# Projections of a chunk in another order, two roots by ACT, and row maxima of the second attention by differences of key blocks

## The reference

```
x = norm(x + attn0(x))      # 16 heads of 64, causal, softmax(q k / 8)
x = norm(x + ffn0(x))       # silu(x w1) * (x w2), two 512x512 layers with gelu, w3
x = norm(x + attn1(x))      # 16 heads of 8, no mask, a Gaussian bias on the scores
x = norm(x + x W^T + b + x (low-rank weight)^T)
```

```
c = tanh(mq @ wfq + bfq + (mean(mq) @ wfg + bfg));  P = 2048 * sigmoid(sum(c*up));  Z = 2048 * sigmoid(sum(c*uz))
G = -2 (j - P)^2 / Z^2                     # for key position j, per head and query
probs = softmax(q k / sqrt(8) + G);  ctx = probs v
```

## Time and profile before

| | |
|---|---|
| median of 3 runs | 1779.66 us (1779.0 to 1783.94) |
| the profiled execution | 1781.96 us, span 1780.2 us |
| PE busy | 1620.0 us (91%) |
| DVE busy | 1313.4 us (74%) |
| ACT busy | 983.8 us (55%) |
| POOL busy | 719.3 us (40%) |

### The profile page before, as it was taken

One profiled execution on the slowest core, in us unless ns is written; L12 is line 12 of the kernel. 1 busy time (PEld: TensorE's weight loads), 2 busy tenths in 40 slices (PEclk: granted clock), 3 DMA queues, 4 the chain that ended last, 5 costly groups with the idle time before them and its releaser, 6 DMA issues. The chain is left out here.

```text
span 1780.2 us, 28289 instructions
## 1 busy us (share of the span) xinstructions
PE 1620.0 (91%) x10680; PEld 477.6 (27%) x10680; DVE 1313.4 (74%) x2616; ACT 983.8 (55%) x1168; POOL 719.3 (40%) x462
## 2 busy tenths in 40 slices
PE   7899999999999999995988579999999999999995
PEld 3232333333332323222444211111111111111122
DVE  6767576666667575723555589999999999999964
ACT  2444545544545544442545306777777777777774
POOL 4577887878787878895222110000000000000012
PEclk8999999999999999996999758999999999999998
DMA  5100000000000000001012430111211121111000
GB/s 113 37 8 13 14 13 8 13 14 7 19 8 19 8 13 14 13 13 26 8 36 58 128 68 1 24 24 24 46 30 31 30 39 24 24 24 24 2 2 24
DMA packets 76217, 46.42 MB, mean 26 GB/s; under 512 B 22158, under 2 KB 74930, under 8 KB 76082
## 3 DMA queue, kind: packets, MB, share of 16 engines
q1 hardware_dynamic: 74738, 43.38, 11.4%
q10 hardware_dynamic: 1344, 1.25, 0.2%
HBM read 25.66 MB, written 9.31 MB: 20 GB/s over the span
## 5 line engine op out<-in xcount | busy, mean ns | idle before, releaser
L1899 DVE TENSOR_REDUCE maxpart<-ps_r 128x1 f32<-128x512 f32 x1024 | 634.4, 682 | 24.8 <-PE ps_r L1757 23.1
L1716 ACT ACTIVATE probs<-ps_e 128x1024 f32<-128x1024 f32 x512 | 504.8, 1023 | 193.1 <-PE ps_e L1785 187.9
L369 POOL TENSOR_TENSOR acc<-acc,probs 128x1024 f32<-128x1024 f32 (+3 forms) x256 | 503.2, 1965 | 77.6 <-ACT probs L422 56.1
L422 ACT ACTIVATE probs<-ps_e 128x1024 f32<-128x1024 f32 (+1 forms) x320 | 285.7, 901 | 371.0 <-PE ps_e L591 124.9
L1757 PE MATMUL ps_r<-krows,qrows 60*128 60x512 bf16 x1024 | 346.8, 402 | 50.5 <-DVE maxpart L1899 17.9
L608 PE MATMUL ps_o<-probs,v 128*64 128x512 f32 (+3 forms) x1280 | 307.6, 559 | 0.2 <-ACT pv_raw L429 0.2
L1681 POOL TENSOR_TENSOR rstd<-veps,power 128x4 f32<-128x4 f32 x8 | 8.1, 1012 | 698.5 <-DVE veps L1949 698.5
L698 DVE TENSOR_REDUCE maxpart<-ps_x 128x2 f32<-128x1024 f32 x192 | 234.5, 1221 | 74.7 <-PE ps_x L516 74.7
L1785 PE MATMUL ps_e<-qrows,krows 62*128 62x512 bf16 x1024 | 278.6, 386 | 2.3 <-ACT probs L1716 0.9
L1795 PE MATMUL ps_o<-probs,v 128*9 128x512 f32 x2048 | 269.5, 598 | 12.4 <-ACT probs L1716 12.3
L1757 PEld LDWEIGHTS ps_r<-krows,qrows 60*128 60x128 bf16 x1024 | 79.9, 94 | 468.2 <-DVE maxpart L1899 352.6
(11 more groups left out here) (305 smaller groups left out, 1396.1 us busy)
## 6 DMA issues: line engine op xcount, KB each, us to landing
qrows<-q_rows SPq DMA_DIRECT2D x64, 192.0 KB
rbc<-rden SPq DMA_DIRECT2D x128, 64.0 KB, 2.1
q_rows<-parts_q SPq DMA_DIRECT2D x24, 128.0 KB, 2.3
k_rows<-parts_k SPq DMA_DIRECT2D x24, 128.0 KB, 2.3
krows<-k_rows SPq DMA_DIRECT2D x16, 192.0 KB, 5.4
w_rows<-parts_w SPq DMA_DIRECT2D x6, 256.0 KB, 2.6
qrows<-a_rows SPq DMA_DIRECT2D x64, 24.0 KB
qrows<-w_rows SPq DMA_DIRECT2D x64, 24.0 KB
```

The lines of the kernel that those rows point to most:

```text
L369: pool.tensor_tensor(acc[:, u % 2, :, o:], acc[:, u % 2, :, o:], probs[:, turn % RING, :, o:], ALU.add)\
L422: act.activation(probs[:, turn % RING, :, o:], ps_e[:, turn % 2, :, o:], ACT.Exp, scale=1.0 / math.sqrt(D0))\
L1716: act.activation(probs[:, HG * (turn % 2) + hh], ps_e[:, e % 2], ACT.Exp).then_inc(s_ex, 1)
L1899: dve.reduce_max(maxpart[:, at:at + 1], ps_r[:, k, :], AX.X).then_inc(s_bf[k], 1)
```

## The change

1. **Projections.** The four projections of a chunk run in the order q, k, f, v in place of q, k, v, f. q stands ahead of `hidden(c, 1, (0, 1))`, k behind it, f behind the third block of that layer, and v behind the fourth. ACT empties q ahead of the first gelu of the layer and f ahead of the last. DVE takes `value` behind the last `hidden_low`, not ahead of it.
2. **Roots.** For the first layer norm of the stage and the last one, ACT takes a square root (`square_root`) and DVE the reciprocal of it, in place of POOL's power. The other six norms of the stage keep POOL.
3. **Maxima.** For chosen pairs of key blocks A = b (upper rows) and B = b + 1 (lower rows), PE computes q (kA - kB) in one matmul over 124 rows, with `nrows` holding kA and -kB; ACT writes relu of it to `over`; DVE adds `over` to the scores of B and takes the maximum in one instruction (`tensor_tensor_reduce`), since max(A, B) = B + relu(A - B). Blocks 8 to 71 of the stretch before the first turn are all paired (32 pairs); from then on the first of the four pairs of each turn (119 turns). In a turn the blocks go in the order 0, 2, 3, 1, 4, 5, 6, 7, where 0 is the difference and 1 the block that joins it; ACT's relu stands behind the exponential of head 0.
4. **What that needs.** The 4 unused rows of `qrows` and of `nrows` are set to 0 by 4 DMAs each from a row that DVE clears; `nrows` is filled by ACT (negation, 60x4096) and POOL (copy) for the first head group, and by POOL (both) for the other three; `maxpart` is set to -3e38 once. The low-rank weight's copies on ACT stand between the relus.

The core of the diff:

```diff
-        J_AT = {(kind, c): 4 * c + n for c in range(NQ) for n, kind in enumerate("qkvf")}
+        J_AT = {(kind, c): 4 * c + n for c in range(NQ) for n, kind in enumerate("qkfv")}
...
                 if c + 1 < NQ:
                     to_tokens("n0", c + 1)
+                if c > 0:
+                    project("q", c - 1)
                 hidden(c, 1, (0, 1))
                 if c > 0:
-                    project("q", c - 1)
                     project("k", c - 1)
                 hidden(c, 1, (2,))
                 if c + 1 < NQ:
                     to_features("n0", c + 1)
                 if c > 0:
-                    project("v", c - 1)
+                    project("f", c - 1)
                 hidden(c, 1, (3,))
                 if c > 0:
-                    project("f", c - 1)
+                    project("v", c - 1)
...
+            def square_root(n):
+                act.wait_ge(s_ve, n + 1)
+                act.activation(root[:, :], veps[:, :], ACT.Sqrt).then_inc(s_rt, 1)
...
+                if (name, c) in (("n0", 0), ("n1", NQ - 1)):
+                    link(dve.reciprocal(rstd[:, :], root[:, :]))
...
                 hidden_low(c, 1, 2)
                 if c > 0:
                     key(c - 1)
+                hidden_low(c, 1, 3)
+                if c > 0:
                     value(c - 1)
-                hidden_low(c, 1, 3)
...
-            return [("max", b) for b in range(first, min(first + LEAD, NU * BU))]
+            return [("max", first + n) for n in (0, 2, 3, 1, 4, 5, 6, 7) if first < NU * BU]
...
+        DIFF = {b: n for n, b in enumerate([b for b in range(2 * NC, BU + LEAD) if b % 2 == 0] +
+                                           [b for b in range(BU + LEAD, NU * BU) if b % (2 * NC) == 0])}
...
+            def positive(b):
+                n, (k, m) = DIFF[b], RING_OF[b]
+                act.wait_ge(s_bp[k], m + 1)
+                if n >= 2:
+                    k1, m1 = RING_OF[JOINS[n - 2]]
+                    act.wait_ge(s_bf[k1], m1 + 1)
+                act.activation(over[:, n % 2, :], ps_r[:, k, :], ACT.Relu).then_inc(s_bf[k], 1)
...
+            act.wait_ge(s_k[0], 16 * NQ)
+            rows = slice(64, 64 + R_M)
+            act.activation(nrows[rows, 0], krows[rows, 0], ACT.Copy, scale=-1.0).then_inc(s_neg, 1)
...
                 for hh in range(HG):
                     exps(HG * turn + hh)
+                    for op in TURNS[turn][2 * hh:2 * hh + 2]:
+                        if op[0] == "max" and op[1] in DIFF:
+                            positive(op[1])
...
+                    return pe.matmul(out, qrows[0:64 + R_M, u % 3, c, hh, t * P:(t + 1) * P],
+                                     nrows[0:64 + R_M, u // NQ % 2, hh, c * KB:(c + 1) * KB], start=True, stop=True)
...
+                    dve.tensor_tensor_reduce(out=larger[:, n % 2, :], in0=ps_r[:, k, :], in1=over[:, n % 2, :], scale=1.0, scalar=-3e38,
+                                             op0=ALU.add, op1=ALU.max, accum_out=maxpart[:, at:at + 1]).then_inc(s_bf[k], 1)
```

More of the change, by code:

```diff
@@ L881, in build @@
         power = sb("power", [P, 4])
+        root = sb("root", [P, 4])
         rstd = sb("rstd", [P, 4])
@@ L999, in _ @@
                 sp.dma_start(end_w[n][:, :], a[f"L1_{src}"].rearrange("(a n) -> a n", a=1).to_broadcast([P, DM])).then_inc(s_ew, 16)
-            sp.wait_ge(s_cr, 5)
+            sp.wait_ge(s_cr, 6)
+            for row in range(R_M, 64):
+                sp.dma_start(qrows[row:row + 1].rearrange("a u c h (x n) -> a (u c h x) n", n=KB),
+                             zrow[0:1, :, :].to_broadcast([1, 3 * 2 * HG, KB])).then_inc(s_z, 16)
             n_d = 0
@@ L1523, in build @@
         rowmax = sb("rowmax1", [P, HG * 4], F32)
+        nrows = sb("nrows", [P, 2, HG, HALF], BF16)
+        over = sb("over", [P, 2, QC], F32)
+        larger = sb("larger", [P, 2, QC], BF16)
         maxhl = sb("maxhl1", [P, 2, 2, HG * 4], BF16)
@@ L1552, in build @@
         s_bf = [sem(f"s_bf1{k}") for k in range(3)]
+        s_neg = sem("s_neg1")
+        s_cpy = sem("s_cpy1")
         s_rm = sem("s_rm1")
@@ L1627, in _ @@
         def _(sp):
+            for row in range(R_M, 64):
+                sp.dma_start(nrows[row:row + 1].rearrange("a b h (c n) -> a (b h c) n", n=KB),
+                             zrow[0:1, :, :].to_broadcast([1, 2 * HG * HALF // KB, KB])).then_inc(s_z, 16)
             load_g(sp, 1)
@@ L1670, in _ @@
             pool.tensor_tensor(w_t[:, :], w_t[:, :], w_d[:, :], ALU.add).then_inc(s_wt, 1)
+            pool.wait_ge(s_wt, 1)
+            pool.wait_ge(s_xb, NQ)
+            for g in range(1, NG):
+                negate_k(g)
+                copy_k(g)
             steps = [0]
```

62 lines of the change are left out of this document (51 added, 11 removed).

## The result

The changed kernel takes 1766.65 us (median of 4 runs, 1765.82 to 1767.26), the kernel before 1779.34 beside it. The ratio is 0.992, 95% interval 0.9905 to 0.9935: 13 us faster, clear of the 0.3% (5.3 us) that the prediction takes for the least that can be told from no change. The forecast was 1746.6 and its range ended at 1766.0. The sign was right; the size was off by a factor of 2.6.

What follows compares the result with a forecast made beforehand. It took a chain over PE, DVE and ACT, not DVE's amount of work, to bound steady turns. Terms -17.9 - 1.2 - 3.5 - 10.5 = -33.1 on 1781.96 gave 1748.9, less 2.3 for the median 1746.6 us; range 1732 to 1766.

Steps and rivals of the forecast that it cites:

- Projections, -17.9 forecast: Ffn stage: PE's waits for the readers of v and q go, and most of the half clock behind them: -17.9 us.
- Roots, -1.2: First and last layer norm: root and reciprocal at 0.4 replace POOL's 1.01 us power, 0.6 saved twice: -1.2 us.
- part 3: Maxima ahead of the first turn: 28 pairs save 0.16 us each, weight copies take about 1.0 back: -3.5 us.
- The turns, -0.7 a unit: Ring turns: turn 7 and turns 0 to 2 together give -0.7 us a unit, in 15 units -10.5 us.
- the steady chain: Turns 3 to 6: a chain over PE, DVE and ACT sets 5.16 us a turn and keeps all links, so no gain.
- Turn 7's -0.6: End of a unit: one maximum less before the copy of the transposed maxima, so the DMA starts 0.6 us earlier.
- the -0.1 of turns 0 to 2: Start of a unit: DVE no longer decides, but ACT is nearly full and turn 2's equal rows pair less well: -0.1 us.
- Rival A: Units give nothing: ACT's relu costs in turns 0 to 2 what turn 7 gains; -22.6, 1757 us; chance 0.17.
- Rival C: Turns: PE pays for full rows and equal halves side by side, 0.2 us in 119 turns, 1770 us; chance 0.09.
- Rival B: Turns: DVE decides after all, every turn shrinks by 0.45 us, 54 us more gain, 1703 us; chance 0.06.
- D: Turns: DVE waits for the relu and the ring falls behind, +36 on -22.6, slower at 1793 us; chance 0.06.
- E: Ffn stage: projections give a third, their wait replaced by one for `key`; -21, 1758 us; chance 0.08.

Runs made afterwards that it cites:

- e1: The kernel before with the new order of the projections alone: 1763.32 us, ratio 0.9886.
- e2: The kernel before with the two roots by ACT alone: 1783.65 us, ratio 1.0009.
- e8: The changed kernel with a one-column exponential on ACT ahead of the relus, to load its table early: 1763.11 us, ratio 0.9896.
- e7: The changed kernel with the bf16 identity written by ACT, ahead of its negation, in place of DVE's cast: 1763.21 us, ratio 0.9895.
- e9: The kernel before with each turn's first block over full rows, zeros for the negated keys, no relu or join, identity by ACT: 1787.31 us, ratio 1.0031.
- e6: The changed kernel with a turn's blocks in the order 0, 3, 2, 1, 4, 5, 6, 7: 1762.48 us, ratio 0.9891.
- e10: The kernel before with the second half of `pv` ahead of the fifth block in each turn: 1790.27 us, ratio 1.0048.
- e12: The changed kernel without turn 2's difference, identity by ACT, exponential's table early, second half of `pv` ahead of the fifth block: 1762.83 us, ratio 0.9896.

## Why the prediction was wrong

The time is 20.0 us above the forecast. Of these, 16.9 stand in the profiled execution (16.8 by the landmarks): 13.0 in the turns and 4.9 ahead of them, less 1.1 that the ffn stage gave more. The other 3.1 are no mechanism: the profiled execution of the kernel before was 2.3 above its median, which the forecast took off again, and the changed kernel's was 0.8 below.

1. **Projections, -17.9 forecast.** e1 alone has 20.0 at the gate product, counted from the start of the stage, and a first block of the ring 19.1 earlier. The mechanism and the places were right. The clock's fall went away whole; I had left 0.7 of it.
2. **Roots, -1.2.** Each step is 0.63 shorter, as taken, but that is not the stage: up to the gate product e2 keeps 0.01 of it, and the changed kernel is 0.7 ahead of e1. The added loads lie in idle time. The Trainium skill's higher price for a switch (ScalarE: Activation LUTs, What ACT_TABLE_LOAD costs) is not borne out here: the load at tanh starts 0.02 us after the activation ahead of it ends, is 1.28 long, and is followed by the next activation 0.01 later (981.42 to 982.71 in the changed kernel), and nothing waits for it. What I missed belongs to the relus of part 3: the change also moves a load that was there before, the exponential's, from idle time to between a relu and an exponential: 0.9 us of turn 0 (e8).
3. **Ahead of the first turn, -3.5; measured +1.4.** The failed sentence is "Filling `nrows`, on ACT and on POOL, is done beside the first eight blocks". In the changed kernel it is done before them, at 1013.28, and PE's first block starts at 1013.40: a DVE cast of 0.21 us stands still during POOL's copy, and PE waits for the cast, 2.7 us (e7). The first block comes 1.9 us late by it, as that sentence priced a late fill, but by another route. The pair's pitch was right, and by the chain named; the weight steps took 1.7 of it back and not "about 1.0". Up to the first split the balance is +0.3, and 1.1 more are lost from there to the first `pv`, 0.9 of them by the exponential's load (e8).
4. **The turns, -0.7 a unit; measured +0.17 (by the mean unit; the turns as a whole scatter by more, see above).** The claim that the steady chain keeps its links held: 5.16 before and after, with DVE idle. Turn 7's -0.6 came out as -0.4: its first step is 0.52 shorter, and the next, which the DMA ends, some 0.1 longer. The failed term is the -0.1 of turns 0 to 2, which measured +0.56. It took DVE, which runs there without a gap, for the engine that sets their length; with a maximum less for DVE in each, turns 0 and 1 are as long as before (8.61 against 8.59), and turn 2 is longer. The sentence on equal rows priced the pairing at nearly nothing. In turn 2, which has no wait to hide it, the full-row difference costs 0.31 (e9) and the blocks 3 and 1 of equal halves 0.22 (e6). Over 15 units this term is 9.9 us off, turn 7 another 3.

The range was also drawn too narrow for its own sum: the bounds of the four parts add up to 1728 and 1780, and the text has 1733 to 1762 without saying how. The time lies 0.65 us above the range.

Rival A had the right outcome (the units give nothing), and the wrong cause: in the turns of a unit ACT's relu costs nothing that the runs show, since e9 has the same 0.31 without it. Rival C had the right cause at the wrong place: full rows cost their slot once a unit, in turn 2, not in 119 turns, because a steady turn has the wait for the bank to hide them. What it quotes from the Trainium skill (TensorEngine Tiling (Array Packing), Key Properties) is borne out that far: the trace shows a full-row matmul start only near the end of the half-row ones (0.53 in place of 0.23). That the array drains between half rows and full rows beyond that is not needed to explain the numbers. Rival B, DVE deciding every turn, is out: the saved 0.45 us appear as DVE's idle time. Rivals D and E did not come.

The Trainium skill's rule on relu (ScalarE: Activation LUTs, Rules for kernel authors) would have put the relu on DVE. No run here tried it.

What stays open: where the 0.63 us of each root are lost in e2; why the clock falls near 1700 us in some executions and not in others; and the bound of a steady turn. The chain named for it was taken apart in e10 and e12, and the turn became only 0.08 to 0.14 us shorter, so another limit lies close behind it. Which wait closes the turn at 5.02 was not tested.

## What to carry to other kernels

An edit that relieves one engine pays only where that engine is last; price what it takes from the others at the place with the least slack, here the one turn of eight where PE has no wait left to hide a slot. Here matmuls of half the rows ran two at a time, and a full-row one, or two blocks of the same half with one scores between them, broke the pairs: look for the neighbours, not at the instruction alone. When setup work moves onto an idle engine, look at what else runs then on the engines beside it, and at which table load moves with it. And before a step of 0.1 us is multiplied by the number of units, look at whether it is the same in all of them: the step of turn 2 is, and turn 7's is not.
